# Scores of a single key row from VectorE products and an all-ones matmul, the key norm moved ahead in five steps, and the hand-over of the first batch reordered

## The reference, cut to what matters

```python
# x: 16 batches x 56 rows x 256; context: 16 batches x 1500 rows x 256
q     = rms_norm(x_ln @ q_w + q_b, nq_s)                  # 16 heads of 128
k_img = rms_norm(ctx[:, :257] @ ki_w + ki_b, nki_s)       # 257 image keys
k_txt = rms_norm(ctx[:, 257:] @ k_w + k_b, nkt_s)         # 1243 text keys
out   = softmax(q k_img' / sqrt(128)) v_img + softmax(q k_txt' / sqrt(128)) v_txt
x     = x + out @ o_w + o_b
x     = x + mixture_of_32_experts(layer_norm(x))          # 4 of 32, and a shared one
```

## Time and profile before

| | us |
|---|---|
| median of 3 runs | 1937.68 (1935.91 to 1941.32) |
| the profiled execution | 1937.42 |
| its span, first to last instruction | 1935.3 |
| mean granted TensorE clock | 0.970 |
| TensorE's first matmul of `attend` | at 255.06 |
| last sums of `attend` | at 1459.26 |

### The profile page before, as it was taken

One profiled execution on the slowest core, in us unless ns is written; L12 is line 12 of the kernel. 1 busy time (PEld: TensorE's weight loads), 2 busy tenths in 40 slices (PEclk: granted clock), 3 DMA queues, 4 the chain that ended last, 5 costly groups with the idle time before them and its releaser, 6 DMA issues. The chain is left out here.

```text
span 1935.3 us, 30607 instructions
## 1 busy us (share of the span) xinstructions
PE 1774.7 (92%) x8863; PEld 1563.6 (81%) x8863; DVE 1328.5 (69%) x2522; ACT 977.4 (51%) x1627; POOL 1099.4 (57%) x955
## 2 busy tenths in 40 slices
PE   7899969999999999999999999999992998699998
PEld 7566769889888898898898898898882887588887
DVE  4444457877877777777777768777772565577776
ACT  3444435555655655655555555556552563244443
POOL 1000267778778787788788787787862331133332
PEclk9999989999999999999999999999996999699999
DMA  3355555455555565554464564555435782133332
GB/s 109 126 201 198 193 166 117 109 115 123 117 118 119 125 122 116 121 129 121 101 147 101 113 132 120 114 119 124 101 84 189 250 274 86 61 118 108 121 108 78
DMA packets 417215, 251.17 MB, mean 130 GB/s; under 512 B 350123, under 2 KB 368683, under 8 KB 415372
## 3 DMA queue, kind: packets, MB, share of 16 engines
q1 hardware_dynamic: 417164, 250.54, 50.7%
HBM read 187.70 MB, written 60.10 MB: 128 GB/s over the span
## 5 line engine op out<-in xcount | busy, mean ns | idle before, releaser
L1297 ACT ACTIVATE p_high<-psum,key_rms 128x448 fp32r<-128x448 f32 x384 | 245.1, 638 | 393.1 <-PE psum L1128 393.1
L1370 DVE TENSOR_TENSOR p_low<-psum,p_high 128x448 fp32r<-128x448 f32 x384 | 237.7, 619 | 184.4 <-ACT psum L1299 178.9
L1126 PE MATMUL psum<-u_high,c_high 128*128 128x448 f32 x832 | 307.2, 369 | 26.1 <-DVE psum L1381 13.8
L1128 PE MATMUL psum<-u_high,c_low 128*128 128x448 f32 x832 | 305.6, 367 | 0.0
L1127 PE MATMUL psum<-u_low,c_high 128*128 128x448 f32 x832 | 305.2, 367 | 0.0
L1126 PE MATMUL psum<-p_high,c_high 128*128 128x448 f32 (+1 forms) x768 | 283.5, 369 | 4.1 <-DVE p_low L1370 4.1
L1127 PE MATMUL psum<-p_low,c_high 128*128 128x448 f32 (+1 forms) x768 | 282.2, 367 | 0.0
L1128 PE MATMUL psum<-p_high,c_low 128*128 128x448 f32 (+1 forms) x768 | 281.9, 367 | 0.0
L1564 POOL TENSOR_TENSOR c_low<-stage,c_high 128x512 fp32r<-128x512 f32 x208 | 276.7, 1330 | 0.0
L1381 DVE COPY psum<-beta_wide 128x448 f32<-128x448 f32 x416 | 260.9, 627 | 21.7 <-DMA beta_wide<-absorbed_biases 5.8
L1558 POOL TENSOR_TENSOR key_rms<-key_ms,minus_half 128x1 f32<-128x1 f32 x209 | 117.5, 562 | 244.2 <-DVE key_ms L1395 241.8
(11 more groups left out here) (240 smaller groups left out, 3844.4 us busy)
## 6 DMA issues: line engine op xcount, KB each, us to landing
stage<-in_ctx SPq DMA_DIRECT2D x210, 256.0 KB, 2.8
averages<-o_raw SPq DMA_DIRECT2D x64, 448.0 KB, 5.2
o_stage<-averages SPq DMA_DIRECT2D x32, 896.0 KB, 5.6
u_raw<-absorbed_queries SPq DMA_DIRECT2D x60, 448.0 KB, 5.5
absorbed_queries<-u_stage SPq DMA_DIRECT2D x14, 1792.0 KB, 6.8
beta_wide<-absorbed_biases SPq DMA_DIRECT2D x32, 448.0 KB, 5.1
recip_wide<-reciprocals SPq DMA_DIRECT2D x32, 448.0 KB, 4.1
p_wide<-probs_by_expert SPq DMA_DIRECT2D x32, 448.0 KB, 3.6
```

The source lines that it names most:

```text
L1126: nc.tensor.matmul(out, high, rhigh, start=start, stop=False, **kw)
L1128: return nc.tensor.matmul(out, low, rhigh, start=False, stop=stop, **kw)
L1297: nc.scalar.activation(p_high[:, probs_slot(u), :], src, ACT.Exp, scale=key_rms[:, t:t + 1])
L1370: return nc.vector.tensor_tensor(out, a, b, ALU.subtract)
```

## The change

1. **Single image key.** The lone row's values lie on the partitions (`lone_keys`, one extra small load at the start). VectorE multiplies `u_raw` of the two chunks by them and adds (`terms_of_lone`: two instructions for each half, steps 12 and 14 of the batch before), ScalarE rounds (`split_lone`, steps 14 and 16), GpSimd takes the rest (steps 17 and 19), and in steps 4 and 5 two matmuls with the all-ones weight replace the six. For the first batch the three pieces run right ahead of and in steps 1 and 2. SyncE's load of the next image `u` waits for `lone_summed` too.
2. **Norm first in five steps.** In VectorE's program `norm` stands ahead of `take` in steps 2, 4, 6, 8 and 10 instead of 6 alone.
3. **First transfers reordered.** `flip`, `wide` and `flat` move one or two rows of `u` earlier, so that `beta` is ready earlier; the text `beta` is loaded behind head 15's `u`; GpSimd adds 2 to `u_scaled`, `u_high_ready` and `u_split` ahead of the branch instead of behind it.
4. **Semaphores.** Those of `prologue` are kept and cleared by GpSimd at the end of `attend`.

```diff
 order (project)
-            if h == H - 1:
-                order += [("wide", half) for half in range(2)]
             for r in range(4):
-                if h == H - 2 and r == 2:
+                if h == H - 2 and r == 1:
                     order += [("flip",)]
-                if h == H - 1 and r == 1:
+                if h == H - 2 and r == 3:
+                    order += [("wide", half) for half in range(2)]
+                if h == H - 1 and r == 0:
                     order += [("flat",)]
...
-                    first_tiles[6](sp)
+                    first_tiles[6](sp, 0)
...
+            first_tiles[6](sp, 1)
...
-            absorb(H - 2, range(2))
+            absorb(H - 2, range(1))
...
-            absorb(H - 2, range(2, 4))
+            absorb(H - 2, range(1, 3))
...
-            pe.wait_ge(wk_split, H)
-            absorb(H - 1, range(1))
+            absorb(H - 2, range(3, 4))
...
-            absorb(H - 1, range(1, 4))
+            pe.wait_ge(wk_split, H)
+            absorb(H - 1, range(4))
...
+        LONE_TERMS, LONE_HIGH, LONE_LOW = (12, 14), (14, 16), (17, 19)
...
                         if has_next and t == 1:
                             sp.wait_ge(u_split, 4 * it + 2)
+                            sp.wait_ge(lone_summed, 2 * it + 2)
...
-                if half == 0:
+                if t == LONE:
+                    pe.wait_ge(lone_split, 2 * it + half + 1 + CREDIT["lone_split"])
+                elif half == 0:
                     pe.wait_ge(ctx_low, TILES * it + t + 1)
...
+                if t == LONE:
+                    for part in (lone_high, lone_low):
+                        last = nc.tensor.matmul(out, ones_r[:, :], part[:, half, :], start=False, stop=True,
+                                                skip_group_check=True)
...
+            def split_lone(it, half):
+
+                act.wait_ge(lone_summed, 2 * it + half + 1)
+                act.wait_ge(scores_done, UNITS * (it - 1) + 2 * LONE + half + 1 + CREDIT["scores_done"])
+                copy(lone_high[:, half, :], lone_terms[:, half, :]).then_inc(lone_high_ready, 1)
...
+            def terms_of_lone(it, half):
+
+                n, terms = 2 * it + half, lone_terms[:, half, :]
+                dve.wait_ge(u_scaled, 4 * it + half + 1)
+                dve.wait_ge(lone_split, n - 1 + CREDIT["lone_split"])
+                nc.vector.tensor_scalar(terms, u_raw[:, 0, cols_of(half)], lone_keys[:, ds(NC * it, 1)], None, ALU.mult)\
+                    .then_inc(lone_step, 1)
+                dve.wait_ge(lone_step, n + 1)
+                nc.vector.scalar_tensor_tensor(terms, u_raw[:, 1, cols_of(half)], lone_keys[:, ds(NC * it + 1, 1)],
+                                               terms, ALU.mult, ALU.add).then_inc(lone_summed, 1)
...
-                    norms_first = step == 2 * LONE + 2
+                    norms_first = step % 2 == 0 and (step + 1 in TEXT_SUMS + IMAGE_SUMS or step == 2 * LONE + 2)
...
+            def split_lone(it, half):
+                gp.wait_ge(lone_high_ready, 2 * it + half + 1)
+                nc.gpsimd.tensor_tensor(lone_low[:, half, :], lone_terms[:, half, :], lone_high[:, half, :].bitcast(F32),
+                                        ALU.subtract).then_inc(lone_split, 1)
...
             gp.wait_ge(first_split, 9)
+            gp.sem_inc(u_scaled, 2)
+            gp.sem_inc(u_high_ready, 2)
+            gp.sem_inc(u_split, 2)
             with gp.If(unsafe(gp)):
...
-            gp.sem_inc(u_scaled, 2)
-            gp.sem_inc(u_high_ready, 2)
-            gp.sem_inc(u_split, 2)
             batches(gp, body, tail)
+            nc.clear_and_free_semaphores(begun)
```

More of the change, by code:

```diff
@@ L178, in layer_norm, with build @@
     return tensor, scalar, vector, pool, done
[L181 removed]
+def build(nc, xT_in, ctx_in, lone_in, qw_in, kw_in, kwb_in, vw_in, small_in, router_in, bias_in, ffn_in, out):
     ctx = ExitStack()
@@ L674, in scalar @@
                     weights_q(h + 3)
-                if h == H - 1:
+                copy_u(h, range(4) if h != H - 2 else range(3))
+                if h == H - 2:
                     for half in range(2):
@@ L679, in scalar @@
                             .then_inc(wide_copied, 1)
-                copy_u(h, range(4))
+                    copy_u(h, range(3, 4))
                 if h == H - 3:
@@ L738, in vector @@
                           psum[0:ROWS_SQ, SUMS:SUMS + 2, 0:HALF]).then_inc(sums_copied, 1)
-            copy_u(H - 2, range(2))
+            copy_u(H - 2, range(1))
             dve.wait_ge(flipped, 1)
@@ L744, in vector @@
                 .then_inc(bound_step, 1)
-            copy_u(H - 2, range(2, 4))
+            copy_u(H - 2, range(1, 3))
             first_tiles[4](dve)
@@ L752, in vector @@
             V.tensor_reduce(bound_max[:, :], bound_sq[:, :], mybir.AxisListType.X, ALU.max).then_inc(bound_step, 1)
-            copy_u(H - 1, range(1))
+            copy_u(H - 2, range(3, 4))
             dve.wait_ge(bound_flat, 1)
@@ L763, in vector @@
                             q_rms_wide[0:2 * H, :].rearrange("p (h n) -> p h n", h=2), ALU.mult).then_inc(beta_ready, 1)
-            copy_u(H - 1, range(1, 4))
+            copy_u(H - 1, range(4))
         def gpsimd(gp):
@@ L806, in first_loads, with first_betas @@
         def first_loads(sp):
+            sp.dma_start(lone_keys[:, :], lone_in).then_inc(lone_loaded, 16)
             for t in range(PREP + 1):
                 sp.dma_start(stage[:, t, :], ctx_in[t, :, :]).then_inc(ctx_loaded[t], 16)
[L810 to L813, removed]
+        def first_betas(sp, s):
+            sp.dma_start(beta_wide[:, s, :].rearrange("p (h q) -> p h q", h=H),
+                         beta_rows[s, :, 0:S].partition_broadcast(P)).then_inc(beta_loaded[s], 16)
         def first_gram(pe):
@@ L858, in attend @@
         lone_probs = sb("lone_probs", [P, 2, HALF])
+        lone_terms = sb("lone_terms", [P, 2, HALF])
+        lone_high, lone_low = [x_high[:, i, :].rearrange("p (h n) -> p h n", h=2) for i in range(2)]
         p_high, p_low = sb("p_high", [P, P_RING, HALF], F32R), sb("p_low", [P, P_RING, HALF], F32R)
@@ L1151, in scores @@
                 out = psum[:, bank_of(u), 0:HALF]
-                for c in range(NC):
-                    w = slice(c * P, (c + 1) * P)
-                    last = three(out, c_high[:, k, w], c_low[:, k, w], u_high[:, 2 * s + c, cols],
-                                 u_low[:, 2 * s + c, cols], False, True, skip_group_check=True)
+                if t == LONE:
+                    for part in (lone_high, lone_low):
+                        last = nc.tensor.matmul(out, ones_r[:, :], part[:, half, :], start=False, stop=True,
+                                                skip_group_check=True)
+                else:
+                    for c in range(NC):
+                        w = slice(c * P, (c + 1) * P)
+                        last = three(out, c_high[:, k, w], c_low[:, k, w], u_high[:, 2 * s + c, cols],
+                                     u_low[:, 2 * s + c, cols], False, True, skip_group_check=True)
                 if not safe:
@@ L1324, in body @@
                 for step in range(UNITS):
+                    if not has_prev and step in (1, 2):
+                        split_lone(it, step - 1)
                     if has_prev:
@@ L1338, in body @@
                         split_u(it + 1, IMAGE, IMAGE_SPLIT.index(step))
+                    if has_next and step in LONE_HIGH:
+                        split_lone(it + 1, LONE_HIGH.index(step))
             def tail(it):
@@ L1478, in body @@
                         reciprocals(it, IMAGE)
+                    if has_next and step in LONE_TERMS:
+                        terms_of_lone(it + 1, LONE_TERMS.index(step))
             def tail(it):
@@ L1548, in _ @@
                 seed(0, u)
+            dve.wait_ge(lone_loaded, 16)
+            for half in range(2):
+                terms_of_lone(0, half)
             batches(dve, body, tail)
@@ L1636, in body @@
                         scale_first(TEXT, 1)
+                    if not has_prev and step in (1, 2):
+                        split_lone(it, step - 1)
+                    if has_next and step in LONE_LOW:
+                        split_lone(it + 1, LONE_LOW.index(step))
                     if step in (2, 4):
```

41 lines of the change are left out of this document (27 added, 14 removed).

## The result

The changed kernel took 1923.59 us (median of 4 runs, 1921.02 to 1924.43) where the kernel before took 1939.5 in the same series (4 runs, 1935.91 to 1942.01): a ratio of 0.9917, 95% interval 0.9897 to 0.9938. It is faster by 0.8%, and the predicted 1925 is 1.4 us off. The profiled execution took 1923.51 at a span of 1921.7.

What follows compares the result with a forecast made beforehand. TensorE was taken as the bound, except between steps 2 and 8, bound by GpSimd's chain with VectorE's norms. 1937.4 - 7.5 + 1.6 - 6.6 = 1924.9, so 1925 us; range 1888 to 1936, likeliest case 1915 to 1932.

Steps and rivals of the forecast that it cites:

- Matmuls taken out: Steps 4 and 5: eight fewer matmuls, 1.64 us a batch, worth nothing except as far as GpSimd's chain gets shorter.
- Norm first: Steps 2, 8 and 10: gaps ahead of the sums close, the blocked split takes much back; 0.5 us a batch left.
- Its size: The norm order's gain over fifteen batches, all but the first: -7.5 us.
- The added pieces: Single-key work in steps 12 to 19, priced at nothing; 2.1 us a batch if GpSimd's slack is missing.
- first batch: The lone row's pieces enter GpSimd's already bound chain there: +1.6 us, bounds 0 and 2.1.
- Hand-over: From projection to `scores(0)`: branch off the path, `beta` and head 15's `u` earlier; -6.6 us, bounds -8.5 to -2.2.
- Semaphores: Clears at the kernel's end lie beside the last stores: nothing.
- The sum: Whole kernel: 1937.4 profiled - 7.5 + 1.6 - 6.6 = 1924.9 us; with the median 0.3 higher, 1925.
- No block: Split in steps 2 and 8 not blocked by GpSimd: 3.2 to 3.4 us a batch, 1885 to 1889 us; chance 0.12.
- no second block: Steps 2 and 8: subtraction gets the ports ahead of `c_low`; 2.1 us a batch, 1901 us; chance 0.2.

Runs made afterwards that it cites:

- e2: Changed kernel with the six matmuls each of `scores(4)` and `scores(5)` put back, products kept: 1925.27 us, ratio 0.9933 to the kernel before.
- e8: e4 with the six matmuls each of `scores(4)` and `scores(5)` put back: 1910.45 us, ratio 0.9861 to the kernel before.
- e11: e1 with the six matmuls each of `scores(4)` and `scores(5)` put back: 1930.52 us, ratio 0.9961 to the kernel before.
- e1: Changed kernel with the norm behind `take` again in steps 2, 4, 8 and 10: 1930.59 us, ratio 0.9961 to the kernel before.
- e12: e9 with VectorE's order of e10, so without the single key's edit: 1903.40 us, ratio 0.9825 to the kernel before.
- e4: Changed kernel with VectorE's split of the sum ahead of the norm in steps 2 and 8: 1910.59 us, ratio 0.9858 to the kernel before.
- e5: Changed kernel with VectorE's order norm, split, `take` in steps 2 and 8: 1895.43 us, ratio 0.9786 to the kernel before.
- e9: Kernel before plus norm first and the hand-over's new order; no single key's edit, additions behind the branch, old semaphores: 1923.06 us, ratio 0.9916.
- e7: Kernel before with only the norm put ahead of `take` in steps 2, 4, 8 and 10 as well: 1925.08 us, ratio 0.9940.
- e3: Changed kernel with the hand-over's old unit order and `beta` loads, additions still ahead of the branch: 1928.47 us, ratio 0.9945 to the kernel before.
- e10: e5 with the seed of `scores(8)` ahead of the norm in step 6: 1896.63 us, ratio 0.9787 to the kernel before.

## Why the prediction was right

Set the timeline after on that of before at the first cast of the split (786.54 in the earlier trace rows, 781.74 after, so add 4.80), and the working can be checked row by row:

| start of | predicted | after, shifted |
|---|---|---|
| cast of step 2 | 789.99 | 790.12 |
| `c_low`, with its wait for the cast | 791.13 | 791.16 |
| `p_low` of unit 2 | 792.96 | 793.00 |
| `average(2)` | 793.6 | 793.67 |
| norm 3 | 794.68 | 794.71 |
| `scores(8)` | 801.3 | 801.25 |
| norm 5 | 805.7 | 805.61 |
| `p_low` of unit 8 | 810.8 | 810.56 |
| `average(8)` | 811.4 | 811.23 |

- **Matmuls taken out: nothing by itself.** This is shown three times, by e2, e8 and e11 (batches +0.1, -0.3 and +1.5 us for 26 us of matmuls), and by the new gap in e1. e12 bears out the condition that the step named, that it counts as far as the chain gets shorter, with the reserve said there.
- **Norm first.** The mechanism is shown: the gaps ahead of the sums go, and the blocked split gives most of it back at `average(2)` and `average(8)`. e4 and e5 move the split out of GpSimd's way, change no work, and win 13 and 28 us by the medians (11 and 25 by the ratios). In e4 the same work of VectorE stands ahead of `p_low` as in the changed kernel, and the wait for it is gone, so VectorE's load alone is not the cause. By the Trainium skill, page SBUF — State Buffer, section Who interferes with whom, issue order decides who of the two blocks; the traces agree, with 1.33 for the cast behind `u_low`'s start in the changed kernel and 0.38 ahead of it in e5.
- **Its size.** Predicted -7.5 over fifteen batches. Measured: a middle batch went from 75.03 to 74.46, the fourteen behind the first changed by -7.5, and the last by -2.7 (72.97 to 70.33), where I had -0.5. The last batch has no `scale_u` in step 8, so its image split is not blocked and keeps its whole gap; its timeline has 1.50 at `average(2)` and nothing at `average(8)`. I had seen that the blocker there was `scale_u`, and not asked in which batch it is absent.
- **The added pieces: nothing,** and first batch +1.6. The first batch measured +1.5. In the others the single key's edit costs 0.15 where it was priced at nothing (e9 against the changed kernel), and norm first without it is worth 0.70 (e7), not 0.5. The two errors cancel in the sum.
- **Hand-over -6.6.** It is 5.4 between the two profiles; e3 gives 4 to 5 for the order, and the branch 1.3 to 1.9 on top. On the time base of before, less 2.56, `u` landed at 248.1 and not at 247, `scores(0)` came at 249.7 and not at 248.4. The broadcast's issue took 0.41 and not 1.13, but the last `u` was issued at 243.5 and took 4.7 to land, where I had 243.0 and 4.0. That is the term that was mis-sized, by 1.2 in these profiles. Of the branch's 2.16, 1.89 are gone: TensorE starts 1.53 behind the landing, not 3.42.
- **Semaphores: nothing.** In every run of the kernels with this edit the device time is 1.7 to 2.0 us above the span of the instructions, in every run of the four without it (before, e7, e9, e12) 2.1 to 3.6. These four lack the single key's edit as well, so whose doing it is remains open.
- **The sum.** The total is nearer than its parts. Inside the batches -8.7 us were measured where -7.5 + 1.6 had been forecast, at the hand-over -5.4 for -6.6: two errors of 2.8 and 1.2 that partly cancel. And the 1.4 us between 1925 and 1923.59 compare times alone; the step forecast was 12.7 us, the step measured 15.9, since the kernel before came out 1.8 higher in this series. That the sum came so close is in part luck.
- **Rivals.** "No block" and "no second block" are out for the changed kernel by the 1.33 of the cast and the 1.58 of the subtraction. e5, whose split is hardly blocked, shows about what they would have given: its 1895 lies between their 1885 to 1889 and 1901. The 1889 was added up wrongly, though: 3.2 to 3.4 us in each of fifteen batches make 1882 to 1885.

## What to carry to other kernels

A gap that is closed on one engine is worth what the next late thing leaves of it: before moving an instruction forward, look at what its completion starts on the other engines, and whether that gets in the way of the instructions that now stand behind it. Where VectorE and GpSimd work on SBUF at once, put VectorE's casts and two-input instructions between the instruction that starts GpSimd and GpSimd's first long piece: that order alone was worth 25 to 28 us here, more than the whole change. Work taken out beside a bound chain only turns into a gap; measure it again when the chain is shorter, as e12 against e10 suggests. And read the whole difference between two kernels before naming one after an edit: here the branch alone, 1.3 us, stood between kernels that were meant to differ in the single key.

## What the runs showed of the hardware

- When both engines are queued they take turns piece by piece, and neither keeps the other out for good: `u_low`, cast, `c_low`, subtraction, `c_twice` in the changed kernel, with 1.33, 1.44, 1.58 and 0.99 us where each alone takes 0.39, 1.30, 0.63 and 0.73.
- `p_low`, a subtraction with one input in PSUM, takes 0.57 to 0.63 in the changed kernel, whether one of GpSimd's long pieces (over 1.2 us) runs beside it or not, with a median of 0.62 either way. In the same trace the subtraction with two SBUF inputs goes from 0.63 to 1.58.
- The issue of one DMA on SyncE's queue took 3.09, 2.61 and 3.28 us (before, e7, e3) right behind two broadcasts and 0.60 some 1.6 us behind a single one, with the same shape; so the cost of an issue is in part what was queued ahead of it. Number and distance of the broadcasts were not told apart.
- Two executions of the same code up to the row behind the layer norm differ by up to 2.6 us there (32.4 to 35.0), which is about half of the hand-over's worth. A comparison of two profiles needs a common mark behind such a place.
